# TensorE's order in an attention step: the transposes of the probabilities move from the second place to the last

## The chip, the cores and the metric

The kernel runs on one core of a Trainium2 chip. The metric is the device time of one execution in microseconds (us), lower is better. TensorE multiplies matrices and transposes, VectorE, ScalarE and GpSimd do the elementwise work, SyncE issues the DMAs. Each engine works off its own instructions in program order, and the engines wait for each other through semaphores.

## What is computed

The program is a stack of layers over 1024 tokens of width 512: feed-forward, full softmax attention with 32 heads of 128, feed-forward, a second kind of feed-forward, a retrieval attention, and feed-forward again. Only the softmax attention is touched by the change:

```python
q, k = rms_norm(x @ Wq + bq, gq), rms_norm(x @ Wk + bk, gk)      # per token over all 4096 columns
v = x @ Wv + bv
attn = softmax(einsum('bhqd,bhkd->bhqk', q, k) / sqrt(128))       # 32 heads, 1024 x 1024 each
out = einsum('bhqk,bhkd->bhqd', attn, v)
x = x + (out @ Wo + bo)
```

## The kernel before

Every fp32 operand of a product is split into a high part (written by ScalarE as fp32r) and a low part (the rest, by VectorE or GpSimd), and a product is three TensorE matmuls: high by high, high by low, low by high. The helper `product` (L348) issues them; `core.bank(b)` is one of eight PSUM banks of 512 columns.

`attention_block` goes through 256 steps, 8 query tiles of 128 tokens for each of 32 heads. A step p works on four different tiles at once, each a few steps behind the other, and every engine has its part of the step written out in a fixed order. In the words used below, with their lags:

- **scores(p)**: TensorE, 6 matmuls of 512 columns, into one of two pairs of banks (`scores(l)`).
- **max(p)**, **bias(p)**: VectorE, the row maximum of the scores (L1066) and the small `nbias` (L1068).
- **exp(p)**: ScalarE, the probabilities and, with a second short instruction, their sums (L1011).
- **transposes(p-2)** (`T_LAG` = 2): TensorE, 8 transposes of 128 by 128 in two halves of four, into the only pair of transpose banks (`T_BANKS`, L1136).
- **high copies(p-2)**, **low parts(p-2)**: ScalarE (L1004) and VectorE (L1076) take the two halves out of `T_BANKS`.
- **PV** (`PV_LAG` = 6): TensorE, 6 matmuls of the second product, probabilities by V (L1161), a quarter of the sum over keys for a group J of four tiles; a group's sum is complete after four steps.
- **y**: once in four steps (l = 2 and 6 of each 8) ScalarE copies the high part of PV's bank (L996), and VectorE makes the low part (L1062), before their other work of the step. PV of the next group waits for it.
- **output product(p-12)** (`WO_LAG` = 12): TensorE, 3 matmuls by Wo into the only output bank (`WO_BANK`, L348 with the tiles `at_o` and `at_y`).
- **reciprocal(p)** and **add(p-12)**: VectorE, `rsums` from the sums of exp(p) (L1081), and the output bank scaled and added to x (L1090).

TensorE's order in a step before the change is scores(p), transposes(p-2), output product(p-12), PV. It waits for exp(p-2) before scores(p), and before the output product with

```python
wait(pe, s_added, p - WO_LAG)     # add(p-13) is done: WO_BANK is free again
```

ScalarE's order is y when due, high copies(p-2), exp(p), then once a head a copy each for k (l = 1 of 8, 1024 columns, L981), Wo (l = 5, L1025) and v (l = 7). VectorE's order is y's low part when due, max(p), bias(p), low parts(p-2), reciprocal(p), add(p-12), then once a head its work on k and q (l = 0, 3, 4).

The function `steps` runs the 256 steps and 12 more in which only the lagging parts are left; the next block's layer norm begins in these.

Of the kernel before, what the change touches and what calls it, by code (L numbers as in the profile page):

```python
# [13 lines left out]
P = 128  # L14
# [33 lines left out]
def wait(eng, sem, value):  # L48

    if isinstance(value, int) and value <= 0:  # L50
        return
    eng.wait_ge(sem, value)
# [284 lines left out]
def product(nc, out, pairs, start=True, stop=True):  # L337


    terms = []  # L340
    for (sh, sl), (mh, ml) in pairs:
        terms.append((sh, mh))
        if ml is not None:
            terms.append((sh, ml))
        if sl is not None:
            terms.append((sl, mh))
    for n, (s, m) in enumerate(terms):
        last = nc.tensor.matmul(out, s, m, start=(start and n == 0), stop=(stop and n == len(terms) - 1))  # L348
    return last
# [478 lines left out]
def attention_block(core, ins, scratch, following, ahead):  # L828
# [5 lines left out]
    nc = core.nc  # L834
    x = core.x
    T_LAG, PV_LAG, OUT_LAG, WO_LAG = 2, 6, 10, 12
    BODY = 2 * NT
    STEPS = HEADS * NT
    with ExitStack() as ctx:
        def sb(name, shape, dt=F32):  # L840
            return ctx.enter_context(nc.sbuf_tensor(f"at_{name}", shape, dt))

        def sem(name):
            return core.semaphore(f"at_{name}")

        def pair(name, shape):
# [11 lines left out]
        probs = [sb(f"probs{i}", [P, TOK]) for i in range(4)]  # L858
# [6 lines left out]
        s_scores, s_max, s_bias, s_exp, s_rsum = (  # L865
            sem(n) for n in ("scores_done", "max_done", "bias_done", "exp_done", "rsum_done"))
        s_T, s_pT_hi, s_pT_lo = sem("transposed"), sem("pT_hi_done"), sem("pT_lo_done")
# [7 lines left out]
        T_BANKS, PV_BANK, WO_BANK = core.ps[2], 6, 7  # L875

        def scores(l):
            return core.ps[l % 2]

        def steps(eng, step):  # L880

            for l in range(BODY):
                step(0, l)
            with eng.Fori(1, STEPS // BODY - 1) as i:
                for l in range(BODY):
                    step(i, l)
            for l in range(BODY):
                step(STEPS // BODY - 1, l)  # L890
            for l in range(WO_LAG):
                step(STEPS // BODY, l)

        def exists(i, l, lag=0):

            return not isinstance(i, int) or 0 <= BODY * i + l - lag < STEPS
# [4 lines left out]
        def final(i, l):  # L901


            k = BODY * i + l - WO_LAG - (HEADS - 1) * NT if isinstance(i, int) else -1
            return k if k >= 0 else None

        def lagging(i, l, lag):


            m = (l - lag) % BODY  # L910
            return (BODY // 4 * i + (l - lag) // 4), (m // 4) % 2, m // NT, m % 4
# [6 lines left out]
        @block.sync  # L918
        def _(sp):
            def load(dst, src, h, arrived):  # L920
                sp.dma_start(dst, src[bass.ds(h, 1)].rearrange("a p n -> p (a n)")).then_inc(arrived, 16)

            def head(h):


                if not isinstance(h, int) or h >= 1:
                    wait(sp, kn_done, h - 1)
                    load(k_raw[:], scratch["k"], h, k_in)
                    wait(sp, q_lo, h)
                    load(q_raw[:], scratch["q"], h, q_in)  # L930
                wait(sp, v_lo, h)
                wait(sp, v_hi, h)
                load(v_raw[:].rearrange("p t d -> p (t d)"), scratch["v_flat"], h, v_in)
                wait(sp, o_lo, h)
                wait(sp, o_hi, h)
                load(o_raw[:], ins["Wo"], h, o_in)

            head(0)
            head(1)
            with sp.Fori(2, HEADS) as h:  # L940
                head(h)
            prefetch.load(sp)
# [166 lines left out]
        @block.tensor  # L1109
        def _(pe):  # L1110
            def step(i, l):
                p = BODY * i + l
                if exists(i, l):
                    qt, hp = l % NT, l // NT
                    (qh, ql), (kh, kl) = q2[hp], k2[hp]
                    if isinstance(i, int) and 2 * i + hp == 0:
                        kh, kl = core.first.hi, core.first.lo
                    elif qt == 0:
                        pe.wait_ge(k_hi, 2 * i + hp)
                        pe.wait_ge(k_lo, 2 * i + hp)  # L1120
                    if qt == 0:
                        pe.wait_ge(q_hi, 2 * i + hp + 1)
                        pe.wait_ge(q_lo, 2 * i + hp + 1)
                    wait(pe, s_exp, p - 1)
                    s = slice(qt * P, (qt + 1) * P)
                    for n in range(NH):
                        m = slice(n * HALF, (n + 1) * HALF)
                        last = product(nc, scores(l)[:, m], [((qh[:, s], ql[:, s]), (kh[:, m], kl[:, m]))])
                    last.then_inc(s_scores, 1)
                if exists(i, l, T_LAG):  # L1130
                    q = p - T_LAG
                    pe.wait_ge(s_exp, q + 1)
                    for b in range(2):
                        wait(pe, s_pT_lo, 2 * (q - 1) + b + 1)
                        for k in range(4 * b, 4 * b + 4):
                            last = nc.tensor.transpose(T_BANKS[:, k * P:(k + 1) * P],  # L1136
                                                       probs[(l - T_LAG) % 4][:, k * P:(k + 1) * P], core.ident[:])
                        last.then_inc(s_T, 1)
                if exists(i, l, WO_LAG):
                    J, jp, hp, w = lagging(i, l, WO_LAG)  # L1140
                    if w == 0:
                        pe.wait_ge(s_y_lo, J + 1)
                        if jp == 0:
                            pe.wait_ge(o_lo, 2 * i + (l - WO_LAG) // NT + 1)
                    wait(pe, s_added, p - WO_LAG)
                    s = slice(w * P, (w + 1) * P)
                    product(nc, core.bank(WO_BANK), [((y2[jp][0][:, s], y2[jp][1][:, s]),
                                                      (o2[hp][0][:], o2[hp][1][:]))]).then_inc(s_wo, 1)
                if exists(i, l, PV_LAG):
                    J, jp, hp, c = lagging(i, l, PV_LAG)  # L1150
                    if c == 0:
                        pe.wait_ge(s_pT_lo, 8 * J + 8)
                        wait(pe, s_y_lo, J)
                        if jp == 0:
                            pe.wait_ge(v_lo, 2 * i + (l - PV_LAG) // NT + 1)
                    terms = []
                    for k in (2 * c, 2 * c + 1):
                        (vh, vl), (ph, pl) = v2[hp], pT2[jp]
                        terms += [(vh, ph, k), (vh, pl, k), (vl, ph, k)]
                    for n, (a, b, k) in enumerate(terms):  # L1160
                        last = nc.tensor.matmul(core.bank(PV_BANK), a[:, k, :], b[:, k, :], start=(c == 0 and n == 0),  # L1161
                                                stop=(c == 3 and n == len(terms) - 1))
                    if c == 3:
                        last.then_inc(s_pv, 1)
                if final(i, l) is not None:
                    pe.wait_ge(s_exp, STEPS)
                    ln.tensor(pe, final(i, l))

            steps(pe, step)
            for k in range(NT, ln.STEPS):  # L1170
                ln.tensor(pe, k)
# [582 lines left out]
```

## Time and profile before

| | |
|---|---|
| median of 3 runs | 2364.14 us (2362.04 to 2364.63) |
| the profiled execution | 2360.17 us, span 2358.3 us |
| attention steps in the profile | from 660 us to about 1800 us |
| TensorE busy | 2279.7 us, 97% of the span |
| VectorE, ScalarE, GpSimd busy | 1639.2, 1095.7, 754.8 us |

The span is the time between the first and the last record of the profiled execution. PE is TensorE's matmul part, DVE VectorE, ACT ScalarE. A matmul's record overlaps the next one, so a group's busy time is that of the union of its records, and the distance between two starts says what one costs. PEclk 1.00 is TensorE's full clock, 2.4 GHz, and 0.50 is 1.2 GHz.

### The profile page before, as it was taken

The numbers are of one execution on the slowest core, as the hardware profiler recorded it, in microseconds if no ns is written. First come the engines' busy times: TensorE is split into PE (matmuls) and PEld (weight loads), VectorE is DVE, ScalarE is ACT, GpSimd is POOL, SyncE is SP. The second block draws the span as 40 slices with busy tenths as digits, with TensorE's granted clock in tenths as the row PEclk, the third lists the DMA queues.
The fourth block names the chain that finished last, engine by engine and source line by source line (L and its number), as shares of the span: only waits on it lengthen the run. The fifth ranks groups of instructions, "written<-read, shape, count | busy, mean of one in ns | idle before, by whom it ended". The sixth has DMA issues, their size and how long they took to land. (4 is left out here: it accounts for less than half of the span.)

```text
span 2358.3 us, 34122 instructions
## 1 busy us (share of the span) xinstructions
PE 2279.7 (97%) x11044; PEld 1867.9 (79%) x11044; DVE 1639.2 (70%) x2677; ACT 1095.7 (46%) x1782; POOL 754.8 (32%) x705
## 2 busy tenths in 40 slices
PE   7799999999979999999999999999998999899998
PEld 5678888888768888888888888888886788687887
DVE  5533333333379999999999999999986565784665
ACT  3222222222156666666666666666663343352442
POOL 5533322222321111112112111111113466572465
PEclk9999999999999999999999999999999999899999
DMA  2234434344221111111111111111101121131210
GB/s 98 100 136 147 142 136 147 130 146 147 103 85 64 44 50 62 53 40 62 53 40 62 59 34 62 62 40 54 63 23 41 40 77 43 33 124 39 72 58 37
DMA packets 91493, 177.42 MB, mean 75 GB/s; under 512 B 8096, under 2 KB 40864, under 8 KB 87968
## 3 DMA queue, kind: packets, MB, share of 16 engines
q1 hardware_dynamic: 91424, 176.54, 21.8%
q8 instruction: 39, 0.64, 0.1%
q14 instruction: 30, 0.25, 0.0%
HBM read 124.08 MB, written 52.43 MB: 75 GB/s over the span
## 5 line engine op out<-in xcount | busy, mean ns | idle before, releaser
L1004 ACT ACTIVATE at_pT_hi<-ps 128x512 fp32r<-128x512 f32 x512 | 278.3, 597 | 253.0 <-PE ps L1136 252.8
L348 PE MATMUL ps<-ln_xT_hi,ln_xT_lo 128*128 128x512 f32 x1488 | 382.0, 392 | 0.0
L1011 ACT ACTIVATE at_probs<-ps,at_nbias,rms 128x1024 f32<-128x1024 f32 x256 | 309.3, 1208 | 147.9 <-DVE at_nbias L1068 145.1
L348 PEld LDWEIGHTS ps<-ln_xT_hi,ln_xT_lo 128*128 128x128 f32 x1488 | 279.5, 188 | 62.8
L1076 DVE TENSOR_TENSOR at_pT_lo<-ps,at_pT_hi 128x512 fp32r<-128x512 f32 x512 | 326.9, 680 | 1.6 <-ACT at_pT_hi L1004 1.6
L1066 DVE TENSOR_REDUCE at_maxes<-ps 128x1 f32<-128x1024 f32 x256 | 311.4, 1216 | 17.6 <-PE ps L348 15.7
L773 POOL TENSOR_TENSOR qkv_acc<-qkv_acc,qkv_sq 128x512 f32<-128x512 f32 x128 | 165.3, 1292 | 342.7 <-ACT qkv_sq L682 341.4
L1136 PE MATMUL ps<-ident,at_probs 128*128 128x128 f32 x2048 | 265.3, 272 | 3.7 <-DVE at_pT_lo L1076 3.7
L1136 PEld LDWEIGHTS ps<-ident,at_probs 128*128 128x128 f32 x2048 | 238.1, 140 | 38.5 <-issue 5.3
L682 ACT ACTIVATE qkv_sq<-qkv_res 128x512 f32<-128x512 f32 x128 | 80.9, 632 | 372.1 <-DVE qkv_res L737 369.4
L348 PE MATMUL ps<-ln_xT_hi,qkv_w_hi 128*128 128x512 f32 x496 | 197.4, 398 | 12.7 <-DVE qkv_res L737 12.7
L1161 PE MATMUL ps<-at_pT_hi,at_v_hi 128*128 128x512 f32 x512 | 205.6, 402 | 2.5 <-DVE at_y_lo L1062 1.7
L1161 PE MATMUL ps<-at_pT_hi,at_v_lo 128*128 128x512 f32 x512 | 201.2, 393 | 0.0
L1161 PE MATMUL ps<-at_pT_lo,at_v_hi 128*128 128x512 f32 x512 | 199.1, 389 | 0.0
L1090 DVE SCALAR_TENSOR_TENSOR x<-ps,at_rsums,x 128x512 f32<-128x512 f32 x256 | 192.0, 750 | 9.9 <-PE ps L348 3.1
L348 PE MATMUL ps<-ln_xT_hi,qkv_w_lo 128*128 128x512 f32 x496 | 197.1, 397 | 0.0
L348 PE MATMUL ps<-ln_xT_lo,qkv_w_hi 128*128 128x512 f32 x496 | 197.1, 397 | 0.0
L948 POOL TENSOR_TENSOR at_o_lo<-at_o_raw,at_o_hi 128x512 fp32r<-128x512 f32 x32 | 41.1, 1286 | 456.4 <-ACT at_o_hi L1025 456.4
L948 POOL TENSOR_TENSOR at_v_lo<-at_v_raw,at_v_hi 128x1024 fp32r<-128x1024 f32 x32 | 76.8, 2401 | 236.5 <-ACT at_v_hi L986 236.5
L948 POOL TENSOR_TENSOR ln_xT_hi<-kn,ln_xT_hi 128x1024 fp32r<-128x1024 f32 x31 | 74.2, 2395 | 202.3 <-ACT ln_xT_hi L981 202.3
L348 PE MATMUL ps<-ln_xT_hi,first_hi 128*128 128x512 f32 x296 | 120.0, 405 | 7.4 <-DVE ln_xT_lo L229 4.0
L348 PE MATMUL ps<-at_o_hi,at_y_hi 128*128 128x512 f32 x256 | 121.7, 475 | 4.7 <-DVE x L1090 4.3
(250 smaller groups left out, 4655.1 us busy)
## 6 DMA issues: line engine op xcount, KB each, us to landing
scratch_q<-qkv_res SPq DMA_DIRECT2D x64, 256.0 KB, 2.0
scratch_k<-qkv_res SPq DMA_DIRECT2D x64, 256.0 KB, 2.0
scratch_v<-qkv_res SPq DMA_DIRECT2D x64, 256.0 KB, 2.3
k_raw<-scratch_k SPq DMA_DIRECT2D x32, 512.0 KB, 4.1
q_raw<-scratch_q SPq DMA_DIRECT2D x32, 512.0 KB, 5.1
at_v_raw<-scratch_v SPq DMA_DIRECT2D x32, 512.0 KB, 3.2
qkv_w<-in_Wq SPq DMA_DIRECT2D x8, 1024.0 KB, 4.9
qkv_w<-in_Wk SPq DMA_DIRECT2D x8, 1024.0 KB, 4.9
```

Source lines behind the costliest of these rows:

```text
L348: last = nc.tensor.matmul(out, s, m, start=(start and n == 0), stop=(stop and n == len(terms) - 1))
L682: nc.scalar.activation(sq[:, u % 2, :], res[u % 4][:], ACT.Square).then_inc(sq_done, 1)
L773: nc.gpsimd.tensor_tensor(part, part, sq[:, u % 2, :], ALU.add).then_inc(acc_done, 1)
L948: nc.gpsimd.tensor_tensor(dst, a, b, ALU.subtract).then_inc(done, 1)
L1004: nc.scalar.activation(pT2[jp][0][:, 4 * b:4 * b + 4, w * P:(w + 1) * P], T_BANKS[:, b * HALF:(b + 1) * HALF].rearrange("p (k n) -> p k n" ...
L1011: nc.scalar.activation(probs[l % 4][:], scores(l)[:], ACT.Exp, bias=nbias[:, l % 4:l % 4 + 1], scale=rq[:, l % NT:l % NT + 1], accum_out=s ...
L1066: nc.vector.reduce_max(maxes[:, l % 4:l % 4 + 1], scores(l)[:], AX.X).then_inc(s_max, 1)
L1076: nc.vector.tensor_tensor(pT2[jp][1][out], T_BANKS[:, b * HALF:(b + 1) * HALF].rearrange("p (k n) -> p k n", k=4), pT2[jp][0][out], ALU.su ...
L1090: nc.vector.scalar_tensor_tensor(out=x[:, tile, :], in0=core.bank(WO_BANK), scalar=rsums[:, c:c + 1], in1=x[:, tile, :], op0=ALU.mult, op1 ...
L1136: last = nc.tensor.transpose(T_BANKS[:, k * P:(k + 1) * P], probs[(l - T_LAG) % 4][:, k * P:(k + 1) * P], core.ident[:])
L1161: last = nc.tensor.matmul(core.bank(PV_BANK), a[:, k, :], b[:, k, :], start=(c == 0 and n == 0), stop=(c == 3 and n == len(terms) - 1))
```

## The change

TensorE's eight transposes of tile p-2, with their two waits, are issued at the end of the step instead of right after the scores. TensorE's order becomes scores(p), output product(p-12), PV, transposes(p-2). No other engine's program changes, and no instruction is added or removed.

```diff
                     last.then_inc(s_scores, 1)
-                if exists(i, l, T_LAG):
-                    q = p - T_LAG
-                    pe.wait_ge(s_exp, q + 1)
-                    for b in range(2):
-                        wait(pe, s_pT_lo, 2 * (q - 1) + b + 1)
-                        for k in range(4 * b, 4 * b + 4):
-                            last = nc.tensor.transpose(T_BANKS[:, k * P:(k + 1) * P],
-                                                       probs[(l - T_LAG) % 4][:, k * P:(k + 1) * P], core.ident[:])
-                        last.then_inc(s_T, 1)
                 if exists(i, l, WO_LAG):
...
                     if c == 3:
                         last.then_inc(s_pv, 1)
+                if exists(i, l, T_LAG):
+                    q = p - T_LAG
+                    pe.wait_ge(s_exp, q + 1)
+                    for b in range(2):
+                        wait(pe, s_pT_lo, 2 * (q - 1) + b + 1)
+                        for k in range(4 * b, 4 * b + 4):
+                            last = nc.tensor.transpose(T_BANKS[:, k * P:(k + 1) * P],
+                                                       probs[(l - T_LAG) % 4][:, k * P:(k + 1) * P], core.ident[:])
+                        last.then_inc(s_T, 1)
```

## Rows read from the trace of the kernel before

**Rows 1.** Busy time in three stretches: us, each engine's busy time (instructions), PEclk, DMA share, GB/s.
```profile
709.40:1765.70 1056.30, 1055.35 (x5576) 879.75 (x5575) 965.20 (x1604) 675.58 (x1120) 183.59 (x91) 1.00 0.15 52
665.00:685.00 20.00, 13.82 (x75) 10.33 (x76) 16.66 (x29) 14.77 (x25) 5.76 (x3) 1.00 0.08 27
2041.00:2045.50 4.50, 4.48 (x11) 3.51 (x12) 3.79 (x8) 0.20 (x1) 0.51 (x2) 0.50 0.00 0
```

**Rows 2.** Waits from 709 to 1765 us: total us, times, longest.
```profile
ACT at_pT_hi L1004 <- PE ps L1136: 243.5, 199, 2.0
```

**Rows 3.** Timeline of all engines, 1764 to 1775.3 us: start, us, instructions [idle before].
```profile
1764.09 1.54 PE L348 MATMUL ps<-ln_xT_hi,ln_xT_lo 128*128 128x512 f32 x6
...
1765.46 1.03 PE L1136 MATMUL ps<-ident,at_probs 128*128 128x128 f32 x8
1765.66 1.22 DVE L1066 TENSOR_REDUCE at_maxes<-ps 128x1 f32<-128x1024 f32 x1 [0.51 <-PE ps L348]
1766.10 1.09 ACT L1004 ACTIVATE at_pT_hi<-ps 128x512 fp32r<-128x512 f32 x2 [1.84 <-PE ps L1136]
1766.25 0.47 PE L348 MATMUL ps<-at_o_hi,at_y_hi 128*128 128x512 f32 x1
...
1766.92 0.21 DVE L1068 TENSOR_SCALAR at_nbias<-at_maxes,rms 128x1 f32<-128x1 f32 x1
1767.03 0.40 PE L1161 MATMUL ps<-at_pT_hi,at_v_hi 128*128 128x512 f32 x1
...
1767.17 1.21 ACT L1011 ACTIVATE at_probs<-ps,at_nbias,rms 128x1024 f32<-128x1024 f32 x1
...
1768.28 0.19 ACT L1011 ACTIVATION_READ_ACCUMULATOR at_probs<-ps,at_nbias,rms 128x1 f32 x1
1768.41 1.03 PE L1136 MATMUL ps<-ident,at_probs 128*128 128x128 f32 x8
1768.50 0.16 DVE L1081 RECIPROCAL at_rsums<-at_sums 128x1 f32<-128x1 f32 x1 [0.17 <-ACT at_probs L1011]
1768.61 0.75 DVE L1090 SCALAR_TENSOR_TENSOR x<-ps,at_rsums,x 128x512 f32<-128x512 f32 x1
...
1771.66 1.04 PE L1136 MATMUL ps<-ident,at_probs 128*128 128x128 f32 x8
...
1774.13 0.74 DVE L1090 SCALAR_TENSOR_TENSOR x<-ps,at_rsums,x 128x512 f32<-128x512 f32 x1
...
1774.93 0.50 PE L348 MATMUL ps<-at_o_hi,at_y_hi 128*128 128x512 f32 x1
```

**Rows 4.** Timeline of ScalarE in an early step, exp right behind the high copies.
```profile
670.78 1.07 ACT L1004 ACTIVATE at_pT_hi<-ps 128x512 fp32r<-128x512 f32 x2
671.74 1.21 ACT L1011 ACTIVATE at_probs<-ps,at_nbias,rms 128x1024 f32<-128x1024 f32 x1
```

**Rows 5.** Timeline around a y behind the copy for k, and the copy for Wo.
```profile
1115.50 0.19 ACT L1011 ACTIVATION_READ_ACCUMULATOR at_probs<-ps,at_nbias,rms 128x1 f32 x1
1115.59 1.05 ACT L981 ACTIVATE ln_xT_hi<-kn 128x1024 fp32r<-128x1024 f32 x1
...
1116.54 0.59 ACT L996 ACTIVATE at_y_hi<-ps 128x512 fp32r<-128x512 f32 x1
...
1117.15 0.69 DVE L1062 TENSOR_TENSOR at_y_lo<-ps,at_y_hi 128x512 fp32r<-128x512 f32 x1 [0.58 <-ACT at_y_hi L996]
...
1117.99 0.47 PE L1161 MATMUL ps<-at_pT_hi,at_v_hi 128*128 128x512 f32 x1
...
1133.12 0.62 ACT L1025 ACTIVATE at_o_hi<-at_o_raw 128x512 fp32r<-128x512 f32 x1
```

**Rows 6.** Timeline of TensorE at step 12, the first that has an output product.
```profile
706.30 1.03 PE L1136 MATMUL ps<-ident,at_probs 128*128 128x128 f32 x8
```

## The prediction

> **What bounds the kernel now.** I read the busy time by stretches first, to find the stage and its bound. From the first add to the last max, 1056.30 us, PE is busy for 1055.35 us and VectorE for 965.20 us, at PEclk 1.00 [rows 1]. So in the steady part of the attention TensorE is the bound and waits for nobody, but VectorE is only some 9% behind it. Then the list of waits: the long one in this stretch is ScalarE's high copies waiting for the transposes, 243.5 us in 199 places [rows 2]. The reader should see that the copies already start as soon as the transposes allow, so moving the transposes moves the copies. Last the timeline, for who waits for whom inside a step. In step 255 [rows 3]: scores start at 1764.09, transposes at 1765.46 (1.37 us later), output product at 1766.25 (0.79), PV at 1767.03 (0.78), the next transposes at 1768.41 (1.38). The four parts make 4.32 us. From the transposes of step 12 at 706.30 [rows 6] to those of step 255 at 1765.46 [rows 3] are 1059.16 us for 243 steps, 4.36 us a step: PE's four parts and almost nothing else.
>
> **The change, part by part.** No work is added, so what counts is who is held up by the later transposes. Everything that follows them on ScalarE is: ScalarE's order is high copies(p-2), then exp(p). Behind exp(p) stand, on VectorE, reciprocal(p) and then add(p-12). And TensorE's output product(p-11), in the next step, waits for add(p-12), because there is one output bank. Before, the transposes were issued 2.16 us earlier in the step (1766.25 to 1768.41, output product and PV [rows 3]), and the add was done by 1769.36, just ahead of the output product. After, only scores(p+1) stand between the transposes(p-2) and the output product(p-11) that waits for their whole consequence. This closes a loop once a step: output product, PV, transposes, high copies, exp, reciprocal, add, output product of the next step. Its length, link by link:
>
> - transposes start to high copies start: 1765.46 to 1766.10, 0.64 us (the second half follows while the first is copied) [rows 3];
> - high copies start to exp start: 0.96 us, with nothing between [rows 4];
> - exp start to the end of its sums: 1767.17 to 1768.28 + 0.19, 1.30 us [rows 3];
> - to the reciprocal 0.03, to the add 0.11, the add 0.75: 0.89 us [rows 3];
> - end of the add to the output product's first matmul: 0.06 us at 1774.87 to 1774.93 [rows 3], and from the end of y's low part at 1117.84 to PV at 1117.99 0.15 us [rows 5]. I take 0.10 between them;
> - output product 0.78 and PV 1.38 [rows 3].
>
> The sum is 0.64 + 0.96 + 1.30 + 0.89 + 0.10 + 0.78 + 1.38 = 6.05 us a step. The transposes and the scores (0.79 + 1.37 = 2.16 us) lie in the 3.89 us between transposes start and next output product, so TensorE stands idle for some 1.7 us a step behind the scores.
>
> Can another input of exp be later still? Max and bias of the next step follow the add and take from 1765.66 to 1767.13, 1.47 us [rows 3]. Even with a head's extra work of some 1.3 us and y's low part of 0.69 us ahead of them they are done 3.5 us after the add, and exp starts 0.10 + 0.78 + 1.38 + 0.64 + 0.96 = 3.86 us after it. They are hidden. The low parts lie beside exp, as now. Scores(p+1) need exp(p-1), a whole step old. DMAs and GpSimd's parts have longer steps and lose nothing; if one weren't hidden it would show as a wait at a head's first scores.
>
> Around y the loop is a bit longer. PV of a new group needs y's low part, and y's high copy stands on ScalarE behind the previous exp and whatever follows that. Behind the copy for k (l = 1, y at l = 2) PV starts 1117.99 - 1115.69 = 2.30 us after the sums' end [rows 5]; in the new loop it would be due at 0.89 + 0.10 + 0.78 = 1.77 us. That is 0.53 us, and with the longer first matmul after a wait (0.47 for 0.40 us [rows 3, 5]) 0.60 us, for the 29 heads whose y lies in the loop. Behind the copy for Wo, which is 0.43 us shorter (1.05 and 0.62 [rows 5]), it is 0.10 + 0.07, 0.17 us, 31 times. Together 17.4 + 5.3 = 23 us.
>
> The sum against the profiled execution's own time:
>
> - 243 steps at 6.05 us are 1470.2 us, in place of 1059.2: +411.0;
> - y: +23;
> - entry: the first transposes in the loop (step 12) come behind output product and PV: +2.2. Steps 6 to 11 have no output product, and the loop isn't closed there: 0, bounded by 2 us either way;
> - the end: steps 256 and 257 have transposes but no exp. From the transposes at 1765.46 to 1768.41 (2.95 us) becomes 6.05. The next gap, 1768.41 to 1771.66 (3.25), becomes transposes to add, 1771.66 to 1774.87 (3.21), plus 0.10 + 0.78 + 1.38, 5.47 us [rows 3]: +5.3. What follows hangs on that same add and stays.
>
> That is +441.5 us on 2360.2, so 2801.7 us. The three runs' median is 4 us above the profiled execution, and I forecast 2805 us. Bounds: the unknown 0.06 to 0.15 us after the add is -10 to +12 us over 243 steps; links that hold in one step only (0.96 of exp, 0.11 of the add) may be 0.1 us off in all, 24 us either way; y may cost nothing or twice as much, 23 us. The forecast's own range is 2760 to 2865.
>
> **The clock.** TensorE's idle time is what could make it worse. Before the steady part, from 665 to 685 us, it was busy for 13.82 of 20 us, idle between groups in every step, and the granted clock was 1.00 [rows 1]. In the new loop it would be busy for about 4.4 of 6.05 us, 73%, more than those 69%. The clock was at 0.50 from 2041 to 2045.5 us [rows 1], behind a pause of several us. [...]
>
> **The rivals.**
>
> - *The clock falls in the loop.* For it: a pause in each of 243 steps, for a thousand us, where the row shows 20. Against it: that row. Price: at 0.50, 11 matmuls took 4.48 us, 0.41 each [rows 1] in place of 1.38 / 6 = 0.23. Nine in the loop cost 1.6 us more, and the first half of the transposes some 0.6 (an estimate: twice 0.64): 8.3 us a step, 243 x 2.25 = 550 us more, about 3360 us. Chance 0.06, with mixtures of both clocks.
> - *The pause is shorter or longer than the loop says*, because ScalarE and VectorE slow down or speed up each other when their work falls together differently (copies, low parts, exp and max all read PSUM), by 0.3 us or more a step: 2880 and more, or 2730 and less. Chance 0.08.
> - *The other side: the wait is covered.* TensorE would reach the output product no later than the add is done, and the step stays 4.32 us: 243 x 4.32 = 1050, some 9 us less than now, 2351 to 2364 us; VectorE's and TensorE's waits at the low parts would be gone, too. It decides at 2.16 us from transposes start to the add's end, the time of transposes and scores; the links above give 3.79. It would need more than 1.6 us of them not to be in series. Chance 0.02: 0.01 faster, 0.01 the same.
>
> The forecast holds the rest, 0.84. A range of 2755 to 2875 takes in its own range and a little of the second rival, and leaves out about 2 in 10. A change of under 0.2% is no more than this kernel's measurement can tell from none. Faster 0.01, same 0.01, slower 0.98.
>
> **What would show it.** In the changed profile: 6.05 us from one step's transposes to the next; PE busy at 70 to 75% from step 13 on, with one pause of 1.6 to 1.8 us between scores and output product, ended by VectorE's add (L1090); exp starting right behind the high copies, no longer ended by the bias; the low parts, not max, ending by ScalarE's copies; PEclk 1.00. A second, small pause at PV (L1161) at l = 2, ended by y's low part. I am wrong if the pause is at another place, if exp waits for the bias still (then VectorE sets the step), or if PEclk falls below 1.00 for long.

## The result, and the profile after

| | before | after |
|---|---|---|
| median | 2363.2 us (4 runs, 2362.04 to 2364.63) | 2826.8 us (4 runs, 2820.68 to 2833.49) |
| the profiled execution | 2360.17 us | 2820.81 us |

The ratio is 1.196, with a 95% interval of 1.1942 to 1.1978: the changed kernel is slower by a fifth. The forecast was 2805 us, with a range of 2755 to 2875. Two of the changed kernel's four runs took 2821 us and two 2833 us, at a mean granted clock of 0.987 to 0.989 and of 0.982 to 0.984; the profile is of the first kind, and where the clock was lower in the others stays open.

In the changed kernel the transposes are at L1162, PV at L1152; the other lines are those of before. First the busy time of the steady part, with the columns of [rows 1]. The stretch starts where the one before started, 10 us ahead of the first add, and ends where the exp of step 255 starts.

```profile
709.40:2219.40 1510.00, 1138.02 (x5634) 868.51 (x5632) 993.91 (x1619) 659.26 (x1135) 183.41 (x91) 1.00 0.11 36
```

From the exp of step 12 to that of step 255 it is now 1501.3 us, and was 1059.2: 442 us more. TensorE's busy time went from full to 75%, and no other engine is near its limit (VectorE 66%). When no engine is full, look for a loop of waits. The list of waits of the same stretch, from 718 us on, names the links of this one (us in total, times, longest):

```profile
ACT at_pT_hi L1004 <- PE ps L1162: 843.6, 242, 4.3
...
DVE at_pT_lo L1076 <- ACT at_pT_hi L1004: 385.2, 243, 2.2
PE ps L348 <- DVE x L1090: 361.3, 243, 1.9
...
DVE at_rsums L1081 <- ACT at_probs L1011: 93.1, 243, 0.4
...
PE ps L1152 <- DVE at_y_lo L1062: 10.1, 29, 0.4
```

TensorE waits for the add 243 times, once in each of the steps 13 to 255, where before it never did in this stretch. ScalarE's wait for the transposes, the one of [rows 2], went from 243.5 to 843.6 us. ScalarE's wait for the bias (132.9 us, 190 times before) has left the list, and PV waits for y's low part 29 times, once a head. The timeline of all engines over one step answers to [rows 3] (the inner matmuls of the output product and of PV, and the max and bias beside them, are left out):

```profile
1301.27 0.75 DVE L1090 SCALAR_TENSOR_TENSOR x<-ps,at_rsums,x 128x512 f32<-128x512 f32 x1
...
1302.07 0.50 PE L348 MATMUL ps<-at_o_hi,at_y_hi 128*128 128x512 f32 x1 [1.43 <-DVE x L1090]
...
1302.88 0.40 PE L1152 MATMUL ps<-at_pT_hi,at_v_hi 128*128 128x512 f32 x1
...
1304.25 1.03 PE L1162 MATMUL ps<-ident,at_probs 128*128 128x128 f32 x8
1304.88 1.08 ACT L1004 ACTIVATE at_pT_hi<-ps 128x512 fp32r<-128x512 f32 x2 [3.76 <-PE ps L1162]
1305.04 1.64 PE L348 MATMUL ps<-ln_xT_hi,ln_xT_lo 128*128 128x512 f32 x6
1305.52 1.29 DVE L1076 TENSOR_TENSOR at_pT_lo<-ps,at_pT_hi 128x512 fp32r<-128x512 f32 x2 [2.12 <-ACT at_pT_hi L1004]
1305.86 1.21 ACT L1011 ACTIVATE at_probs<-ps,at_nbias,rms 128x1024 f32<-128x1024 f32 x1
1306.95 0.21 ACT L1011 ACTIVATION_READ_ACCUMULATOR at_probs<-ps,at_nbias,rms 128x1 f32 x1
1307.19 0.16 DVE L1081 RECIPROCAL at_rsums<-at_sums 128x1 f32<-128x1 f32 x1 [0.38 <-ACT at_probs L1011]
1307.29 0.75 DVE L1090 SCALAR_TENSOR_TENSOR x<-ps,at_rsums,x 128x512 f32<-128x512 f32 x1
...
1308.19 0.47 PE L348 MATMUL ps<-at_o_hi,at_y_hi 128*128 128x512 f32 x1 [1.51 <-DVE x L1090]
```

Follow the loop by the starts: transposes 1304.25, high copies 1304.88 (0.63), exp 1305.86 (0.98), end of its sums 1307.16 (1.30), end of the add 1308.04 (0.88), output product 1308.19 (0.15; one step earlier 0.05, after an add that ended at 1302.02), PV 0.81 later, the next transposes 1.37 after that. The scores in between are over by 1306.7 and TensorE then stands still for 1.5 us. I had said 1.6 to 1.8 us; most of the difference is how far the last scores' record reaches into the pause.

### The profile page after: what moved, and what is told of

It reads as the page before. It is cut to its first block and busy times, and to the rows that moved or that the text cites. A ratio compares the mean times of both kernels' runs of the same rounds, so it can differ in the third digit from the quotient of the medians.

```text
span 2819.0 us, 34122 instructions
## 1 busy us (share of the span) xinstructions
PE 2359.7 (84%) x11044; PEld 1854.2 (66%) x11044; DVE 1660.3 (59%) x2677; ACT 1071.3 (38%) x1782; POOL 754.1 (27%) x705
## 5 line engine op out<-in xcount | busy, mean ns | idle before, releaser
L348 PE MATMUL ps<-at_o_hi,at_y_hi 128*128 128x512 f32 x256 | 127.9, 500 | 372.8 <-DVE x L1090 372.6
L348 PE MATMUL ps<-ln_xT_hi,ln_xT_lo 128*128 128x512 f32 x1488 | 406.0, 408 | 0.0
L348 PEld LDWEIGHTS ps<-at_o_hi,at_y_hi 128*128 128x128 f32 x256 | 48.0, 187 | 480.3 <-DVE x L1090 438.9
L348 PEld LDWEIGHTS ps<-ln_xT_hi,ln_xT_lo 128*128 128x128 f32 x1488 | 261.1, 189 | 43.8
L1162 PE MATMUL ps<-ident,at_probs 128*128 128x128 f32 x2048 | 268.2, 274 | 2.2 <-DVE at_pT_lo L1076 2.2
L1162 PEld LDWEIGHTS ps<-ident,at_probs 128*128 128x128 f32 x2048 | 241.1, 141 | 37.5 <-issue 4.0
L1152 PE MATMUL ps<-at_pT_hi,at_v_hi 128*128 128x512 f32 x512 | 205.9, 402 | 15.4 <-DVE at_y_lo L1062 13.4
L1152 PE MATMUL ps<-at_pT_hi,at_v_lo 128*128 128x512 f32 x512 | 202.1, 395 | 0.0
L1152 PE MATMUL ps<-at_pT_lo,at_v_hi 128*128 128x512 f32 x512 | 201.0, 393 | 0.0
```

The source lines that it names most:

```text
L1162: last = nc.tensor.transpose(T_BANKS[:, k * P:(k + 1) * P], probs[(l - T_LAG) % 4][:, k * P:(k + 1) * P], core.ident[:])
```

## The experiments

To compare steps, I take the interval from one exp to the next out of each timeline, for steps 13 to 255, 243 intervals, by the step's place l in a group of eight. All in us:

| kernel | mean | median | l = 2 | l = 6 | PEclk, 750 to 1700 us |
|---|---|---|---|---|---|
| before | 4.36 | 4.36 | 4.87 | 4.44 | 1.00 |
| after | 6.18 | 6.12 | 6.67 | 6.20 | 1.00 |
| scores of 4 matmuls | 6.83 | 6.66 | 6.67 | 7.60 | 0.89 |
| scores of 12 matmuls | 6.18 | 6.12 | 6.67 | 6.20 | 1.00 |
| half of the transposes last | 5.70 | 5.64 | 6.19 | 5.71 | 1.00 |
| transposes third | 4.78 | 4.74 | 4.87 | 4.67 | 1.00 |
| add first | 4.99 | 4.32 | 7.76 | 6.20 | 0.97 |
| low parts last | 6.66 | 6.12 | 8.76 | 8.72 | 0.95 |
| low parts last, scores of 12 | 6.38 | 6.12 | 7.22 | 7.17 | 1.00 |
| PV ahead of the output product | 5.57 | 4.75 | 8.81 | 8.26 | 0.96 |
| transposes third and add first | 4.34 | 4.32 | 4.87 | 4.45 | 1.00 |
| before and add first | 4.33 | 4.43 | 4.87 | 4.44 | 1.00 |

The columns l = 2 and l = 6 are medians. PEclk is the mean granted clock. Where single intervals are counted below, the clock is said to have fallen in one if its mean from exp to exp is under 0.97.

**Is the step set by TensorE's work or by the loop?** Twice I changed the amount of work in the scores, which lie outside the loop. First less of it; the products with the low part of q are left out, so the scores are less exact:

```diff
-                        last = product(nc, scores(l)[:, m], [((qh[:, s], ql[:, s]), (kh[:, m], kl[:, m]))])
+                        last = product(nc, scores(l)[:, m], [((qh[:, s], None), (kh[:, m], kl[:, m]))])
```

> The changed kernel with the scores made of 4 matmuls in place of 6 (the low part of q is left out of the scores). Loop theory (output product, PV, transposes, high copies, exp, reciprocal, add, output product): the scores lie in the pause, so the two matmuls saved, 0.46 us a step, only make the pause longer; step 6.1 to 6.2 us, total within 10 us of the changed kernel (2811 to 2835). Rival, the step is set by how much TensorE has to do: 256 x 0.46 = 118 us less, about 2705.

It took 2975.6 us, ratio 1.2591 to before (1.2565 to 1.2617): less work, and 150 us slower than the changed kernel. Neither theory had that. TensorE's timeline shows a step of each kind:

```profile
1502.76 0.78 PE L348 MATMUL ps<-at_o_hi,at_y_hi 128*128 128x512 f32 x1 [1.88 <-DVE x L1090]
1503.33 0.63 PE L348 MATMUL ps<-at_o_lo,at_y_hi 128*128 128x512 f32 x1
...
1506.51 1.03 PE L1162 MATMUL ps<-ident,at_probs 128*128 128x128 f32 x8
...
1510.52 0.50 PE L348 MATMUL ps<-at_o_hi,at_y_hi 128*128 128x512 f32 x1 [2.04 <-DVE x L1090]
1510.85 0.39 PE L348 MATMUL ps<-at_o_lo,at_y_hi 128*128 128x512 f32 x1
...
1512.69 1.03 PE L1162 MATMUL ps<-ident,at_probs 128*128 128x128 f32 x8
```

In the first, output product and PV take 3.75 us (1502.76 to 1506.51), with matmuls of 0.63 us; in the second 2.17 us, with matmuls of 0.39. From those transposes to the next, 1506.51 to 1512.69, is 6.18 us: at the full clock the loop is as long as in the changed kernel, as the loop theory says. But the granted clock in this kernel is 0.89. Counted from one exp to the next, it stayed at 1.00 in 137 of the 243 intervals, which are 6.18 us on average, and fell to the lower of its two levels for a part of the other 106, which are 7.68 us. These 106 account for 159 us, the whole loss. The pause ahead of the output product is alike in both, 1.94 and 1.96 us on average, so its length alone doesn't say in which step the clock falls. Was it the pause, longer than in the changed kernel, or the missing matmuls? The opposite change answers both questions:

```diff
-                        last = product(nc, scores(l)[:, m], [((qh[:, s], ql[:, s]), (kh[:, m], kl[:, m]))])
+                        for _ in range(2):
+                            last = product(nc, scores(l)[:, m], [((qh[:, s], ql[:, s]), (kh[:, m], kl[:, m]))])
```

> The changed kernel with the scores computed twice (12 matmuls in place of 6, the second set over the first; the result is the same). Loop theory: the six extra matmuls (1.38 us) just fit into the pause, which was 1.42 to 1.51 us, so the time stays: 2810 to 2835, with PEclk at 1.00 or above the changed kernel's. Rival, the step is set by TensorE's work: 256 x 1.38 = 353 us more, about 3175. And of the four-matmul run (2976 us, granted clock 0.89 in the attention): if its loss came from the clock in the longer pause and not from the scores, this run, with nearly no pause, must not show such a loss.

2825.9 us (2825.28 to 2826.54): six more matmuls a step, 1.38 us of TensorE's time, cost nothing. The busy time, above of the changed kernel and below of this one, each over the same 950 us, shows where they went:

```profile
750.00:1700.00 950.00, 713.80 (x3530) 544.53 (x3531) 626.23 (x1018) 412.78 (x709) 117.71 (x58) 1.00 0.11 37
```

```profile
750.00:1700.00 950.00, 923.31 (x4451) 717.25 (x4450) 630.23 (x1017) 413.12 (x709) 117.67 (x58) 1.00 0.11 37
```

TensorE is busy for 97% in place of 75%, and the other engines do the same number of instructions in the same time. A TensorE that looks full here is not the bound.

**Which link?** The low parts also follow the transposes and stand ahead of the add on VectorE. In the next run they go behind it (the part `if exists(i, l, T_LAG)` of VectorE's step moves below the part with the add):

```diff
 max(p), bias(p)
-low parts(p-2)
 reciprocal(p), add(p-12)
+low parts(p-2)
```

> The changed kernel with VectorE's order max, bias, reciprocal, add, low parts (before: low parts ahead of the reciprocal). Loop theory: the low parts (1.3 us) lie beside exp, the step is set by exp, reciprocal and add, so nothing changes: 2805 to 2850. Rival, the low parts are the link between the transposes and the add: up to 1.3 us a step less, 2510 and more.

2940.9 us (2940.68 to 2941.17), beyond the range. In the six steps of eight without y the interval is 6.05 to 6.15 us, as in the changed kernel, so the low parts are no link of the loop, and that much of the expectation held. What I hadn't reckoned is in the steps with y, 8.7 us. The timeline of TensorE and VectorE there (the add is L1081 in this kernel, the low parts L1093):

```profile
1426.41 1.28 DVE L1093 TENSOR_TENSOR at_pT_lo<-ps,at_pT_hi 128x512 fp32r<-128x512 f32 x2
1426.55 0.51 PE L348 MATMUL ps<-at_o_hi,at_y_hi 128*128 128x512 f32 x1 [1.51 <-DVE x L1081]
...
1427.61 0.68 DVE L1062 TENSOR_TENSOR at_y_lo<-ps,at_y_hi 128x512 fp32r<-128x512 f32 x1
1428.39 0.73 PE L1152 MATMUL ps<-at_pT_hi,at_v_hi 128*128 128x512 f32 x1 [0.86 <-DVE at_pT_lo L1093]
1428.92 0.63 PE L1152 MATMUL ps<-at_pT_lo,at_v_hi 128*128 128x512 f32 x1
```

PV of a new group pauses for 0.86 us, right behind the output product and its pause of 1.51 us. The row puts that down to the low parts, but these had ended by 1427.69; y's low part, which stands behind them on VectorE, ended at 1428.29, 0.10 us ahead of PV. So the low parts delay PV through y. PV then runs at the lower clock, though not each time: in 43 of the 61 intervals at l = 2 and 6 the clock fell, in the other 18 it stayed at 1.00 and they take 7.2 us. A run with both edits, the low parts last and the scores doubled, separates the two costs:

> The run with the low parts last (2941 us, granted clock 0.93 to 0.98 in the attention), with the scores computed twice, so that TensorE's pause is filled. Theory: the loss against the changed kernel has two parts, a wait of PV for the low parts once in four steps (0.86 us in the trace, 2 in 8 steps, some 50 us) and slow matmuls after the longer pauses. With the pause filled the second part goes: 2870 (2840 to 2890). Rival, the order of VectorE alone makes the whole loss: 2941 or more.

2877.5 us (2877.38 to 2877.7), PEclk 1.00, steps with y 7.2 us. So the wait costs 2877.5 - 2825.9 = 52 us and the clock 2940.9 - 2877.5 = 63 us, by two runs of each kernel.

**How long is the loop?** If the sum of links is right, taking a known link out must shorten it by just that. Half of the transposes stay behind the scores:

```diff
 scores(p)
+transposes(p-2), first four
 output product(p-12)
 PV
-transposes(p-2), all eight
+transposes(p-2), last four
```

> Half of the change: the first four transposes of a tile stay right behind the scores, the other four come last in the step. Loop theory: transposes to high copies 0.64, one copy 0.48 in place of 0.96, exp 1.30, reciprocal and add 0.89, 0.10, output product 0.78, PV 1.38: 5.57 us a step, 294 us more in 243 steps, with y and the end about 325: 2685 (2660 to 2710). Rival, the pause goes with the number of transposes moved and half of them cost half: 2595. Rival, the last transpose is what counts and all is lost: 2820.

2696.0 us (2695.57 to 2696.4), median step 5.64 us, against 6.12: 0.48 less, the one high copy that no longer stands in the loop. Now PV is taken out, by placing the transposes ahead of it:

```diff
 scores(p)
 output product(p-12)
+transposes(p-2)
 PV
-transposes(p-2)
```

> TensorE's order scores, output product, transposes, PV. Loop theory: PV (1.38 us) leaves the loop, which has 0.78 + 0.64 + 0.96 + 1.30 + 0.89 + 0.10 = 4.67 us; with the heads' extra work ahead of max about 4.72; against 4.36 before that is 243 x 0.36 = 88 us: 2450 (2430 to 2470). Rival, any place behind the output product costs the same pause: about 2820. Rival, only a place behind PV costs: 2365.

2469.6 us, ratio 1.0451 (1.0431 to 1.047), with a median step of 4.74 us. That is 1.38 us less than 6.12, as much as PV takes. The total is 20 us above the expectation, at the end of its range: the shortest intervals are 4.65 us, about the 4.67 worked out, but those at l = 1, 2 and 5 are 5.03, 4.87 and 4.81, more than the 0.05 us a step that I had put down for the heads' extra work. There exp waits for the bias again: at l = 1 and 2 the timeline has the bias over at 1312.35 and 1317.23 and exp at 1312.39 and 1317.27, so VectorE's extra work ahead of the maximum sets these steps.

**Is it the add?** The direct test opens the loop on VectorE. The add of tile p-12 needs nothing of step p but the output product, so it can stand ahead of the low parts and the reciprocal, which keeps its wait for exp:

```diff
 max(p), bias(p)
+add(p-12)
 low parts(p-2)
 reciprocal(p)
-add(p-12)
```

> The changed kernel with VectorE's order max, bias, add, low parts, reciprocal: the add of the output no longer stands behind exp of its own step. Loop theory: the loop through the output bank is open and the pause ahead of the output product is gone in ordinary steps (4.33 us). But a second loop, through y once in four steps, then shows: transposes, high copies, exp, y's high copy on ScalarE, y's low part, PV, transposes: 0.64 + 0.96 + 1.30 + 0.09 + 0.58 + 0.03 + 0.69 + 0.15 + 1.38 is 5.8 us, 6.35 behind the copy for Wo and 6.8 behind that for k, so about 4.9 us a step on average and 2490 in all (2470 to 2515), with pauses ended by y's low part only. Rival, the pause comes from something else than the add: above 2780. Rival, no second loop: 2365.

2523.0 us, ratio 1.0681 (1.0662 to 1.07). TensorE's order is the changed one, and yet the median step is 4.32 us, as its work alone. The pause ahead of the output product is gone. In its place stands the second loop, at l = 2 (7.76 us) and l = 6 (6.20 us) only. From TensorE's timeline, PV's first matmul of a group at l = 6 and at l = 2:

```profile
1404.12 0.47 PE L1152 MATMUL ps<-at_pT_hi,at_v_hi 128*128 128x512 f32 x1 [1.59 <-issue]
...
1423.75 0.47 PE L1152 MATMUL ps<-at_pT_hi,at_v_hi 128*128 128x512 f32 x1 [1.97 <-DVE at_y_lo L1062]
```

The first is labelled "issue", but y's low part ended at 1404.02, 0.10 us before it, in ScalarE's and VectorE's rows just as at l = 2. The total lies 8 us above the range. At l = 2 I had expected 6.8, and the median is 7.76; PEclk was 0.97 in this run. The trace has both kinds of such a step. The pause ahead of PV is 1.97 us in 28 of the 30 (2.10 and 1.16 in the others); in 20 of these the clock fell, and the interval is 7.96 us on average, in the other 8 it stayed at 1.00 and the interval is 6.66 to 6.68 us. So the second loop alone is a little shorter than worked out, and the clock's part at l = 2 is 26 us, more than the 8 us above the range. A run with the pause filled would have tested that from the other side; there is none.

The second loop was put to a test of its own, with PV ahead of the output product in the changed kernel, where it has the least room:

```diff
 scores(p)
+PV
 output product(p-12)
-PV
 transposes(p-2)
```

> TensorE's order scores, PV, output product, transposes. The first loop has no PV in it: 4.67 us. But PV now waits for y's low part early in the step, with only the scores between it and the transposes: from transposes start, exp's sums end at 2.90, y's low part 1.45 later without a head's copy ahead, 2.30 behind the copy for k and 1.87 behind that for Wo, so at l = 2 PV starts at 5.2 and the next transposes at 5.2 + 1.38 + 0.78 = 7.4, at l = 6 at 6.9; 4.67 to 4.8 elsewhere. Mean (6 x 4.7 + 7.4 + 6.9) / 8 = 5.3 us: 243 x 0.95 = 231 us more, 2600 (2570 to 2640). Rival, PV ahead or behind makes no difference to the changed kernel's loop: 2820. Rival, no second loop: 2440.

2668.3 us (2668.16 to 2668.49), 28 us above the range. The other steps are 4.66 to 4.81 us as worked out, but for 5.02 at l = 1; those with y are 8.81 and 8.26 in place of 7.4 and 6.9. The timeline of such a step:

```profile
1409.77 1.04 PE L1162 MATMUL ps<-ident,at_probs 128*128 128x128 f32 x8
...
1415.12 0.47 PE L1142 MATMUL ps<-at_pT_hi,at_v_hi 128*128 128x512 f32 x1 [2.91 <-DVE at_y_lo L1062]
1415.42 0.56 PE L1142 MATMUL ps<-at_pT_lo,at_v_hi 128*128 128x512 f32 x1
1415.78 0.63 PE L1142 MATMUL ps<-at_pT_hi,at_v_lo 128*128 128x512 f32 x1
...
1418.77 1.10 PE L1162 MATMUL ps<-ident,at_probs 128*128 128x128 f32 x8
```

PV started 5.35 us after the transposes, where 5.2 was expected. PV and output product then took 3.65 us in place of 2.16, because the clock fell behind the pause of 2.9 us. It fell in 33 of the 61 intervals with y; where it stayed at 1.00, most took 7.34 to 7.37 us at l = 2 and 6.86 to 6.90 at l = 6. The wait was forecast right; the clock's part was left out.

**Both loops open.** With the transposes in third place and the add first, neither loop holds:

> TensorE's order scores, output product, transposes, PV, and VectorE's order max, bias, add, low parts, reciprocal. Loop theory: both loops are open. The add doesn't stand behind exp any more, and PV with its wait for y stands behind the transposes. TensorE is the bound again at 4.33 to 4.40 us a step: 2362 (2350 to 2375), about the kernel before. Rival, transposes behind the output product cost something by themselves: 2400 and more.

2355.3 us (6 runs), ratio 0.9970 (0.9958 to 0.9982). The transposes behind the output product cost nothing by themselves. The same edit on VectorE in the kernel before:

> The kernel before with VectorE's order max, bias, add, low parts, reciprocal. TensorE is the bound with or without it (4.36 us a step for 4.32 us of work), so at most 243 x 0.04 = 10 us can be won: 2358 (2350 to 2368). Rival, the low parts come 0.7 us later and the transposes of the next step wait for them: 2400 and more.

2354.8 us (6 runs), ratio 0.9967 (0.9955 to 0.9979). Both are 0.3% faster than the kernel before, and alike. The step is 4.33 to 4.34 us, down from 4.36, with 4.32 us of work on TensorE.

## Why the prediction was right

**The mechanism**, a loop through output bank, transposes, exp and add, is shown from four sides: the 243 waits for the add, the step that doesn't change with six matmuls more, the links that take off what they measure (0.48 and 1.38 us), and the loop that opens when the add leaves it.

**The terms of the sum**, by the profiled executions, 460.6 us in all (span 460.7):

| term | forecast | measured |
|---|---|---|
| 243 steps and y | +411 and +23 | +442.1 (2219.36 - 718.07, less 1767.17 - 708.00, the starts of exp 255 and exp 12) |
| entry, to exp of step 12 | +2.2 | +6.2 |
| the end, from exp of step 255 on | +5.3 | +8.5 |
| work ahead of the attention | 0 | +3.9 |

The steps without y came out at 6.05 to 6.2 us, the shortest as summed. That at l = 1 is 0.15 us longer, because the add of the step before starts 0.26 us behind the reciprocal, in place of the 0.11 us of [rows 3]; those at l = 0 and 4 are 0.05 us longer, at l = 4 because the output product often starts 0.15 us behind the add and not 0.06. y's excess is 6.67 - 6.05 = 0.62 us at l = 2 and 0.15 at l = 6; 0.60 and 0.17 had been worked out.

**Entry**: the step "steps 6 to 11 have no output product, and the loop isn't closed there: 0, bounded by 2 us" was wrong by 4 us. The second loop, through y, is closed as soon as PV has run, and steps 6 to 11 have no cover for it. The interval to exp 10 was 6.66 us and 4.87 before, with PV waiting 3.25 us for y's low part. The interval to exp 6 grew from 2.90 to 5.55 us. There TensorE waits for the low parts of tile 3 in both kernels; before, the transposes came first behind that wait, now PV stands between them (687.35 to 689.24 us), and the granted clock was 0.50 from 688.4 to 691.8 us, behind that wait of 2.04 us.

**Work ahead**: the exp of step 0 starts at 668.39 us in the changed kernel and at 664.54 before. None of the runs changes anything ahead of it, and over all twelve traces it lies between 663.78 and 670.48 us, so these 3.9 us are scatter between executions.

**The end**: here the rest is the clock's. From 2217 to 2261 us the granted clock of the changed kernel was 0.82, and output product and PV took 3.98 us from 2221.70 to 2225.68. From transposes to transposes it was 7.93 us in place of the 6.05 forecast, and from there to the output product 3.98 in place of 3.21: 2.6 of the 3.2 us. The timeline of TensorE there:

```profile
2221.70 0.77 PE L348 MATMUL ps<-at_o_hi,at_y_hi 128*128 128x512 f32 x1 [2.91 <-DVE x L1090]
...
2225.68 1.91 PE L1162 MATMUL ps<-ident,at_probs 128*128 128x128 f32 x8
```

**The rivals.** The wait wasn't covered, by 1.4 to 1.6 us a step. The clock stayed at 1.00 in the loop, as the row from 665 to 685 us had made likely, but with less room than the chance of 0.06 said: mean pauses of 1.49 us ahead of the output product (229.9 us in 154 steps) left it at 1.00, those of 1.96 us (271.8 us in 139 steps) in the run with four matmuls came with 0.89.

## What to carry to other kernels

In a software pipeline written out by hand, a moved instruction isn't judged by its own length but by the loop that it closes: follow what it releases, through every in-order queue, to the first wait on its own engine one step later, and compare that with what lies between. Here 2.16 us of work had to cover 3.79 us. When an engine waits in each step while none is full, look for the instruction in the loop that doesn't need the one it stands behind: moving the add ahead of the low parts and the reciprocal opened the loop without any work more or less (a second loop, through y, then held two steps in eight), and won 0.3% even in the kernel before, where TensorE hardly paused.

## What the hardware showed that I hadn't expected

Taking matmuls away made the kernel slower, 2976 for 2827 us, and giving TensorE 12 matmuls for 4 made it 150 us faster. The granted clock is the difference (0.89 and 1.00): the steps of the kernel with 4 matmuls in which it stayed at 1.00 are as long as the changed kernel's, 6.18 us.

Four of the runs above left their expected range: scores of 4, low parts last, PV ahead of the output product, and add first. All four have one reason. Where PV or the output product follows a pause of 1.9 to 3.0 us, or pauses of 1.5 and 0.9 us in short order, matmuls of 0.63 us appear in place of 0.39 in some of the steps, and each of them lies in the loop. Such a step is longer by 1.3 to 1.6 us on average, while the pause itself is about the same. And it is some of the steps, never all: 106 of 243 in the first run, 43 of 61 in the second, 33 of 61 in the third, 20 of 28 in the last, at pauses that differ by under 0.1 us on average between the steps of either kind. In the changed kernel, with a mean pause of 1.49 us, it was none of 243. What decides between the steps no run here shows, so a forecast for a loop with such pauses has to carry both values.
